# Layers 2 and 3 of a graph network: TensorE's tile steps written out instead of looped

## What is computed

```
msg = feat[src] * weight[:, None]                 # layer 2
neigh_sum = segment_sum(msg, dst)
rst = feat @ W_self.T + b_self + (neigh_sum / deg) @ W_neigh.T + b_neigh

pa = sigmoid(review_feat @ ps_w.T)                # layer 3
h = segment_sum(pa * (weight * cj)[src], dst) * ci
```

## Time and profile before

| | us |
|---|---|
| median of 3 runs (lowest, highest) | 1210.16 (1206.04, 1212.11) |
| span of the profiled execution | 1210.2 |
| PE busy | 975.2 (81%) |
| DVE busy | 949.9 (78%) |
| ACT busy | 578.9 (48%) |
| layer 2, from its first gather to its last scatter | 972.2 to 1074.9 |
| layer 3, the same | 1093.9 to 1197.0 |

### The profile page before, as it was taken

How to read it: one execution, slowest core, us unless ns; L and a number is a source line. 1 busy time by engine, 2 the same in 40 slices (tenths; PEclk the granted TensorE clock), 3 DMA queues, 4 the chain that set the end, 5 groups by cost and what they waited for, 6 DMA issues and landing times.

```text
span 1210.2 us, 32623 instructions
## 1 busy us (share of the span) xinstructions
PE 975.2 (81%) x12003; PEld 730.6 (60%) x12003; DVE 949.9 (78%) x1297; ACT 578.9 (48%) x1404; POOL 651.8 (54%) x446
## 2 busy tenths in 40 slices
PE   4986768878999999999994867776876488947894
PEld 3655547774445444444443767776775478837884
DVE  8988989996666666676657499999997678787876
ACT  6431138884111011111111477787885278847884
POOL 1018888888787877888778888989400000000000
PEclk9988776567999999999996588989887589988998
DMA  7753216663766666676643377778852998847882
GB/s 158 147 136 78 55 35 209 204 206 103 228 186 214 186 197 216 182 213 182 213 114 115 99 272 265 272 265 274 301 199 85 371 387 320 308 169 244 324 306 62
DMA packets 87984, 245.06 MB, mean 202 GB/s; under 512 B 38268, under 2 KB 39068, under 8 KB 87910
## 3 DMA queue, kind: packets, MB, share of 16 engines
q1 hardware_dynamic: 71700, 228.86, 53.9%
q10 hardware_dynamic: 2465, 13.60, 5.0%
q0 software_dynamic: 13744, 1.59, 4.0%
HBM read 176.60 MB, written 66.92 MB: 201 GB/s over the span
## 4 chain that ended last, share of the span: by engine, by line
PE 45%; DVE 31%; issue 16%; ACT 6%; DVEq 1%; ACTq 1%; DMA 0%; SPq 0%
PE ps L1740 24%; PE ps L1546 6%; PE ps L1520 4%; DVE arena L1006 4%; ACT arena L699 3%; PE ps L1692 3%; DVE arena L1015 2%; DVE arena L1092 2%; DVE arena L1020 2%; DVE h_room L1020 2%; PE ps L1471 1%; DVE hl_room L1242 1%; DVE arena L1214 1%; DVE base_room L1242 1%; PE ps L1596 1%
## 5 line engine op out<-in xcount | busy, mean ns | idle before, releaser
L627 POOL DMA_INDIRECT w_table<-wpa,slot_i x425 | 646.3, 1521 | 209.1 <-issue 209.1
L1740 PE MATMUL ps<-arena,hl_room 125*128 125x500 f16 (+1 forms) x1750 | 344.7, 353 | 2.9 <-DVE hl_room L1278 2.0
L1740 PEld LDWEIGHTS ps<-arena,hl_room 125*128 125x128 f16 x1750 | 155.7, 97 | 163.9 <-issue 5.5
L1499 PE MATMUL ps<-arena 125*128 125x128 f16 (+1 forms) x1300 | 140.6, 237 | 59.8 <-ACT arena L673 54.9
L767 ACT ACTIVATE part_room<-ps 128x500 f16<-128x500 f32 (+1 forms) x70 | 38.0, 543 | 311.4 <-PE ps L1740 311.3
L1287 DVE SCALAR_TENSOR_TENSOR part_room<-ps,part_room 128x500 f16<-128x500 f32 (+1 forms) x70 | 43.5, 622 | 123.9 <-ACT part_room L767 123.9
L1503 PE MATMUL ps<-arena 125*128 (+1 forms) x1300 | 135.8, 205 | 0.0
L673 ACT ACTIVATE arena<-ps 128x384 f32<-128x384 f32 x325 | 130.8, 505 | 7.3 <-PE ps L1503 5.3
L1499 PEld LDWEIGHTS ps<-arena 125*128 125x128 bf16 x1300 | 91.2, 104 | 64.7 <-ACT arena L673 52.3
L1503 PEld LDWEIGHTS ps<-arena 125*128 125x128 bf16 x1300 | 114.3, 108 | 0.5
L1034 DVE TENSOR_TENSOR arena<-ps,part_room 128x384 f32<-128x384 f32 x150 | 75.3, 552 | 32.3 <-PE ps L1520 27.5
(11 more groups left out here) (280 smaller groups left out, 1635.8 us busy)
## 6 DMA issues: line engine op xcount, KB each, us to landing
arena<-oht_table SPq DMA_DIRECT2D x38, 832.0 KB, 6.3
h_room<-slot_rows SPq DMA_DIRECT2D x50, 416.0 KB, 3.9
oht_table<-h_room SPq DMA_DIRECT2D x50, 416.0 KB, 3.0
hl_room<-slot_rows SPq DMA_DIRECT2D x25, 832.0 KB
arena<-slot_rows SPq DMA_DIRECT2D x25, 832.0 KB, 4.7
arena<-ohs_table SPq DMA_DIRECT2D x25, 832.0 KB, 6.1
hl_room<-in_edge_attr_dram ACTq DMA_DIRECT2D x17, 750.0 KB
ohs_table<-xs_room SPq DMA_DIRECT2D x25, 448.0 KB
```

The costliest lines, as they stand in the source:

```text
L627: pool.indirect_dma_start(w_table, bass.IndirectOffsetOnAxis(slot_i[:, u:u + 1], 0), wpa[:, u], None).then_inc(S[f"w_out{g % 2}"], 16)
L1499: pe.matmul(ps[:, m % RING, o:o + 2 * D], ohT[:, par, 0, k * L:(k + 1) * L], rhs, start=(i == 0), stop=(i == 1))
L1740: last = pe.matmul(ps[:, c, 0:w], hl[0:P, u, s, :], adj[:, s, c * CH * P:c * CH * P + w], start=(s == 0), stop=(s == T - 1))
```

## The change

`quad_steps` loses its loop and its `start`: all 29 steps are written out, each with whole numbers for s, t and `pair_no`. Nothing else differs.

```
-        def quad_steps(eng, body, start):
-
-            last = LAST
-            for s in range(start):
-                body(s, s % 4, [k for k in range(last + 1) if k <= s], (s - 4) // 2)
-            with eng.Fori(0, (T - start) // 4) as i:
-                for u in range(4):
-                    body(i * 4 + (start + u), (start + u) % 4, range(last + 1), i * 2 + (start + u - 4) // 2)
-            for s in range(T, T + last):
-                body(s, s % 4, [k for k in range(last + 1) if s - k < T], (s - 4) // 2)
+        def quad_steps(eng, body):
+
+            for s in range(T + LAST):
+                body(s, s % 4, [k for k in range(LAST + 1) if 0 <= s - k < T], (s - 4) // 2)
@@
                 if p == "l1":
                     tile_steps(pe, layer1)
                 else:
-                    quad_steps(pe, layer23, 2 * KEPT[-1] + 5)
+                    quad_steps(pe, layer23)
```

## The result

The changed kernel takes 1197.09 us, the median of four runs (1195.63 to 1202.03), against 1210.37 us (1206.04 to 1212.11) for the kernel before: ratio 0.9895, 95% interval 0.9871 to 0.9920. The prediction was 1198.4 us. The span of the profiled execution is 1193.9 us, and its own time 1195.63 us, so 1.7 us lie around a span.

What follows compares the result with a forecast made beforehand. PE was taken to set the pace in the loops of layers 2 and 3, ACT in the written-out steps ahead. The sum was 1210.2 - 15.8 + 3.0 + 1.0 = 1198.4 us, range 1193.5 to 1209.5 us.

Steps and rivals of the forecast that it cites:

- The relief: Tiles 11 to 24 of layers 2 and 3 would run at ACT's pace: 7.68 and 8.11 us less, 15.8 in all.
- The late blocks: Written-out steps of both layers: instruction fetches slow the pace to 3.72 us a tile against 3.58, giving back 3.0 us.
- the first stop: PE's stop at 1015.88 to 1017.25 us stays and makes ACT wait: 0.5 us in each layer, 1.0 us.
- the slow bound: Written-out steps at 6.65 us a block, 4.09 us a tile: 11.1 us given back, 1206.5 us.
- Why blocks are late: Written-out steps: instruction fetches have to pass tables of 832 KB, with DMA engines 0.96 busy against 0.76 in the loop.
- The clock: PE's one fall to 1.2 GHz in each of layers 2 and 3, about 1.4 us each, would go.
- The second rival: Layers 2 and 3: clock falls at two in five stops, 6.4 falls, 9.0 us, giving 1207.4 us; chance 0.18.
- The slower rival: Layers 2 and 3: clock falls behind most of 16 blocks, no gain from 8.4 falls, up to 1220.8 us; chance 0.10.
- The mean case: Layers 2 and 3 together: the forecast's own sum, -11.8 us, giving 1198.4 us; chance 0.52.

Runs made afterwards that it cites:

- loop with fixed weights: Kernel before, loop kept, but the loop's even tiles' scatters read tile 0's table at a fixed address; 1198.09 us, ratio 0.9907.
- small tables: Changed kernel, but in layer 3 three of four gather-table rooms get only the first quarter of their columns; 1197.94 us in one run.
- layer-2-only kernel: Kernel before with only layer 2 written out, layer 3 keeping the loop with register addresses; 1205.04 us in one run.
- second repetition: Changed kernel measured again without an edit, beside the one with all engines written out; 1199.02 us, ratio 0.9909.
- first repetition: Changed kernel measured again without an edit, in five rounds; 1198.93 us, ratio 0.9913.

## Why the prediction was right

**The relief, -15.8 us.** Right as the distance to ACT's pace, too simple as to its cause. The scatters take 1.45 us, and the profile shows 14.8 us of the relief. I had read PE's 41.46 busy of 42.00 us as a limit that lifts until ACT is the next one, and in this profile that held to 0.1 us a tile. But not all of the 15.8 us is the register instructions' doing: by the loop with fixed weights (5.2 and 5.1 us) and by the looped layer 3 without late blocks (5.1 us) they cost about 10 us in both layers. The other 5 to 6 us, an estimate from the difference, are the loop's own late blocks and clock falls in its first round.

**The late blocks, +3.0, and the first stop, +1.0.** Right in sum, wrong in shape, and so in part luck. Eight written-out layers of profiles without another edit in them (three of the changed kernel with two each, layer 2 of the small tables and of the layer-2-only kernel) took 46.12, 47.38, 51.14, 47.57, 50.15, 46.88, 46.66 and 48.66, on average 48.07 us. Against 46.24 that is 1.8 us a layer, 3.7 us in both, where I had 4.0; single layers lie between -0.1 and 4.9. I had spread it as 0.14 us over each tile, from three block lengths with a mean of 6.05 us. But ACT kept its 3.58 us a tile, 5.83 us a block, until the stops that end the last two of the three, so they say little of a lasting pace, and from tile 11 on not every block is late. In truth most tiles take 3.57 us and a few take 3.6 to 7.4, behind one stop of 2.8 or 3.5 us, behind several usual ones, or behind a stop and a clock fall. The 3.7 us hold the falls too, for which the sum had nothing: three stand in these eight layers, at the prediction's 1.4 us each about 1 us of the 3.7 (an estimate). And the stop that ended at 1017.25 us is not at the end of the steps that don't change: by the count of matmuls it stands in step 13, the first of the loop. The row of 6.65 us a block that I used as the slow bound isn't the slowest that there is: the profile has 6.78, and the second repetition 8.15.

**Why blocks are late.** Right: they stand behind table data, as the small tables show, in one execution. By the Trainium skill's rule (Runtime: NRT & Kernel Launch, section Instruction fetch mechanics) the crossing is mostly hidden. That is so here for all eight blocks at 0.56 of the DMA engines, and not so in the stretches at 0.94 and 0.95 with stops of up to 2.80 us.

**The clock.** Here the step "I take it that they go, since the slow scatter behind the stop goes" failed. The profile of the changed kernel has no fall in these layers, but its first repetition has three, the second one, and the loop with fixed weights two, none with register instructions in a scatter near. Each has a stop ahead of it or under way, from 0.7 to 3.5 us; what decides which stop has a fall stays open. In the three profiles of the changed kernel there are 4 falls for 20 stops of over 1 us. The second rival had two in five stops and, for 16 blocks, 6.4 falls an execution; measured are 1.3. So that rival's mechanism is at work, much more weakly than it had, and is a part of the 3.7 us. The slower rival would have needed more than eight.

**The time.** The mean case was -11.8 us; the three comparisons have ratios of 0.9895, 0.9913 and 0.9909, 10.5 to 12.7 us. One mistake of mine doesn't show in it: I took the span of 1210.2 us for the time of its run, but 1.7 to 1.8 us lie around the span in every run here. The profiled run was then by all appearances the one of 1212.11 us, above the median by about as much, and the two cancel. That the median came within 1.3 us of the forecast is closer than the interval of some 3 us either way can tell, and no sign that each term was right.

## What to carry to other kernels

A register instruction ahead of each short matmul cost PE 65 ns here, on 56 for the matmul; count them in the order of the program, weights and moving data alike, and either write the steps out or compute the addresses once and use the registers again (shown for one tile here, and not tried in a loop). Writing out isn't free where tables stream in: each 127 matmuls with their weight loads needed a new block of instructions here, and while tables arrived many of these came 0.3 to 3.5 us late. What that costs is read from PE's lead over the next engine: PE needs 2.97 us a tile (1.45 + 1.52) where ACT needs 3.57, and with these 0.6 us a tile it makes up for most of the stops. The loop isn't free of it either, since its first round is fetched too.

## What was unexpected

- A matmul with its address in a register is as fast as with a fixed one (26 in 1.4 us), when no register instruction stands between; only the 26 instructions cost (3.1 us).
- The loop pays for its blocks as well, in its first round: 1.44 and 2.61 us of stops and a clock fall in layer 3, and a loop without register instructions in its scatters was no faster than written-out steps (0.9907 against 0.9913).
- A block can come 3.45 us late, where the longest such stop in the profile before was 1.37 us.
- ACT and DVE pace the layers at 3.58 us a tile in loops and at 3.43 us written out, and that gain could not be shown in the time.
